# Routed experts of a decoder block: VectorE's split of the next gate weights moves behind the low part of the inner activations

## The reference, cut to what matters

```
router_logits = x_flat @ gate_w.T
top_w, sel = jax.lax.top_k(router_logits, TOPK)          # TOPK = 2, E = 8
top_w = jax.nn.softmax(top_w, axis=-1)
g = jnp.einsum('nd,efd->enf', x_flat, gate_proj)         # D = 512, F_DIM = 352
u = jnp.einsum('nd,efd->enf', x_flat, up_proj)
h = jax.nn.silu(g) * u
eo = jnp.einsum('enf,edf->end', h, down_proj)
out = jnp.einsum('end,ne->nd', eo, tw)
```

## Time and profile before

| | value |
|---|---|
| profiled execution | 3482.6 us, of which the span of the core 3480.8 us |
| median of three timed runs | 3479.44 us (3477.32 to 3481.93) |
| TensorE matmul busy over the span | 3159.6 us (91%) |
| VectorE, ScalarE, GpSimd busy | 2094.4 (60%), 1278.2 (37%), 1450.4 us (42%) |
| mean granted TensorE clock | 0.955 of full speed |
| stretch of the routed experts of layer 1 | about 3075 to 3412 us from the span's start |

### The profile page before, as it was taken

One profiled execution on the slowest core, in us unless ns is written; L12 is line 12 of the kernel. 1 busy time (PEld: TensorE's weight loads), 2 busy tenths in 40 slices (PEclk: granted clock), 3 DMA queues, 4 the chain that ended last, 5 costly groups with the idle time before them and its releaser, 6 DMA issues. The chain is left out here.

```text
span 3480.8 us, 58860 instructions
## 1 busy us (share of the span) xinstructions
PE 3159.6 (91%) x21152; PEld 2638.6 (76%) x21152; DVE 2094.4 (60%) x3767; ACT 1278.2 (37%) x3276; POOL 1450.4 (42%) x1470
## 2 busy tenths in 40 slices
PE   7999999999969999799896999699999999869991
PEld 6887878878847777678685777488888888758881
DVE  5666566576645776421064777556667678645656
ACT  3333333333346666201102333244444444324430
POOL 4454343344422434300153222355555556544445
PEclk9999999999989999789998999799999999979996
DMA  4001016022310111339563112211101001156665
GB/s 172 18 16 51 0 35 232 0 95 102 141 33 24 53 32 57 144 100 340 171 143 115 37 42 63 99 56 34 36 12 47 12 24 43 39 199 223 225 221 157
DMA packets 137872, 317.18 MB, mean 91 GB/s; under 512 B 18425, under 2 KB 30457, under 8 KB 135538
## 3 DMA queue, kind: packets, MB, share of 16 engines
q1 hardware_dynamic: 120194, 274.61, 23.4%
q0 software_dynamic: 15360, 36.25, 3.9%
q10 hardware_dynamic: 2160, 4.21, 0.4%
HBM read 231.07 MB, written 98.04 MB: 95 GB/s over the span
## 5 line engine op out<-in xcount | busy, mean ns | idle before, releaser
L398 POOL TENSOR_TENSOR a_sq<-a_tq,a_sinq 128x256 f32<-128x256 f32 x128 | 150.3, 1194 | 358.4 <-DVE a_tq L474 358.4
L398 POOL TENSOR_TENSOR a_sk<-a_tk,a_sink 128x256 f32<-128x256 f32 x128 | 123.8, 986 | 90.0 <-DVE a_tk L474 90.0
L364 ACT COPY a_probT<-bank 128x512 f32<-128x512 f32 x64 | 37.6, 587 | 328.3 <-PE bank L713 328.3
L411 POOL TENSOR_TENSOR e_sk<-e_tk 128x512 f32<-128x512 f32 x64 | 66.6, 1040 | 204.6 <-DVE e_tk L501 204.6
L353 ACT ACTIVATE e_prob<-bank,e_nb,e_rq 128x128 f32<-128x128 f32 x256 | 113.9, 455 | 86.7 <-DVE e_nb L575 86.7
L348 ACT ACTIVATE a_sm<-a_sm,a_nmax 128x128 f32<-128x128 f32 x256 | 99.8, 391 | 121.7 <-DVE a_nmax L570 121.7
L952 ACT ACTIVATE b_prob<-bank,b_nb 128x128 f32<-128x128 f32 x512 | 139.4, 387 | 11.6 <-DVE b_nb L1148 11.3
L1046 POOL TENSOR_TENSOR d_prob<-d_prob,d_nmax 128x1024 f32<-128x1024 f32 x32 | 64.0, 1999 | 183.3 <-DVE d_nmax L1143 183.3
L2340 POOL TENSOR_TENSOR n_wu_lo<-nw_wu,n_wu_hi 128x1408 fp32r<-128x1408 f32 x23 | 74.0, 3218 | 135.4 <-DVE n_wu_hi L2384 135.4
L496 DVE TENSOR_TENSOR a_kr<-a_kr,a_sk 128x512 f32<-128x512 f32 x64 | 66.4, 1037 | 89.0 <-POOL a_sk L398 89.0
L1145 DVE TENSOR_REDUCE b_nmax<-bank 128x8 f32<-128x1024 f32 x64 | 77.9, 1217 | 68.6 <-PE bank L1289 67.9
(11 more groups left out here) (512 smaller groups left out, 10718.8 us busy)
## 6 DMA issues: line engine op xcount, KB each, us to landing
packed<-all_zero SPq DMA_DIRECT2D x32, 1024.0 KB, 8.3
cw_wg<-in_c_wg SPq DMA_DIRECT2D x32, 512.0 KB
cw_wu<-in_c_wu SPq DMA_DIRECT2D x32, 512.0 KB
cw_wd<-in_c_wd SPq DMA_DIRECT2D x32, 512.0 KB
nw_wg<-in_f_wg SPq DMA_DIRECT2D x23, 704.0 KB
nw_wu<-in_f_wu SPq DMA_DIRECT2D x23, 704.0 KB
nw_wd<-in_f_wd SPq DMA_DIRECT2D x23, 512.0 KB
nw_xe<-packed SPq DMA_DIRECT2D x46, 256.0 KB, 2.7
```

The costliest lines, as they stand in the source:

```text
L364: nc.scalar.copy(probT[:], pP[:, :]).then_inc(act_pt, 1)
L398: step = nc.gpsimd.tensor_tensor(o, i, s, ALU.mult)
```

## The change

VectorE's list for an odd slot is put in another order. Before: `take_x`, `split_gate`, `take_h`, h. After: `take_x`, `take_h`, `split_gate`, h. Even slots have no `split_gate` and stay as they are, as do all other engines, all buffers and all semaphores. In slot 0, which has no `take_h`, and in the last odd slot, which has no `split_gate`, nothing moves.

```diff
@@ -2387,10 +2387,10 @@
                 t = R * i + n
                 if ahead:
                     take_x(*following(i, n, R))
+                if back:
+                    take_h(*preceding(i, n, R))
                 if n % 2 and not (isinstance(i, int) and later(i, n) > LAST):
                     split_gate(*((i, 1) if n == 1 else (i + 1, 0)))
-                if back:
-                    take_h(*preceding(i, n, R))
                 dve.wait_ge(act_g, done(t))
                 dve.wait_ge(pe_u, done(t))
                 nc.vector.tensor_tensor(h[:, n % 2], gate[:, n % 2], pU[n % 2][:, 0:F], ALU.mult).then_inc(v_h, 1)
```

## The result

The changed kernel takes 3463.66 us (median of 6 runs, 3454.95 to 3465.68) where the kernel before, timed beside it, takes 3483.06 us (6 runs, 3477.32 to 3485.33). The ratio is 0.9943, with an interval of 0.993 to 0.9957: **faster by 0.57%, about 20 us**. The forecast was 3460 us; 3459.7 over 3479.44 is the same ratio, 0.9943. In microseconds the forecast lies 3.7 us under the median, since the kernel before came out 3.6 us slower in six runs than in the three of the forecast.

The account below looks back on a forecast made before the run. TensorE was taken to bound the routed experts, held in odd slots by the low part of h; 16.4 + 4.7 - 1.4 = 19.7 us off 3479.44 gave 3460 us, with 3455 to 3469 for 8 in 10.

Parts of the forecast that it names:

- The bound and the term of 16.4 us: Routed experts: TensorE sets the pace; odd slots from slot 3 on shrink to 6.685 us like even ones, gaining 16.4 us.
- Slots 1 and 2, 4.7 us: Start of the routed stage: a 2.8 us wait and the low clock behind it vanish, gaining 4.7 us, at least 2.8.
- The split costs nothing behind GpSimd's order: Odd slots: the gate-weight split at T+4.1 starts 0.96 us ahead of GpSimd's down-weight instruction, keeps the port, costs nothing.
- an L2379 of 1.6 to 1.9 us: Sign on VectorE in odd slots: the gate-weight split starts at T+4.1 and takes 1.6 to 1.9 us.
- the slack of 1.2 us: Margin between the split's end at T+5.7 to 5.8 and TensorE's need of it at T+7.0, next even slot.
- Rival B: Split falls behind GpSimd's down weights at the port and the gate product waits: 3500 us, or 3528; chance 0.07.
- the first case of B: Split stands still for GpSimd's first instruction only; gate product waits 1.9 us in 22 even slots: 42 us lost, 3500 us.
- The loss of 1.4 us to the loads: Loop of up-weight load, high part, y copy, store, next load: late landings give back 1.4 us.
- the ends of 0 and 4.8: Bounds of the loss to late loads: 0 at best, 4.8 us if all eleven unseen landings came at their bound.
- its cases, which were 4.8 and 1.5: Loss to loads if eleven landings came at their bound (4.8 us) or 0.3 us earlier (1.5 us).
- Rival A: Loads set the pace: each landing takes 8.3 us, 20 pairs lose 0.55 us each after 2 us: 3467 us; chance 0.14.
- Rival C: No difference: odd slots are long for another reason; gain under 5 us, 3475 to 3479 us; chance 0.07.

Follow-up runs that it names:

- a1: The changed kernel run again with nothing else altered; ratio to the kernel before 0.9939, slots 3 to 43 in 273.88 us.
- e2: The changed kernel with SyncE issuing the loads for the pair after next ahead of a store; ratio to the kernel before 0.9934.
- e9: The changed kernel with the earlier loads of e2, run a second time; ratio to the kernel before 0.9935.
- e4: The kernel before with the new order in the odd slots n = 1 alone; ratio to the kernel before 0.9985.
- e5: The kernel before with the new order in the odd slots n = 3 alone; ratio to the kernel before 0.9983.
- a2: The kernel before run again with nothing altered; ratio 1.000, slots 1 and 2 in 19.49 us.
- e1: The changed kernel with the split of the gate weights moved one place further back, behind the product h; ratio to the kernel before 1.0065.
- a3: The changed kernel run a third time with nothing else altered; ratio to the kernel before 0.9946, slots 3 to 43 in 277.27 us.
- e3: The kernel before, VectorE's order as it was, with only the earlier loads of e2; ratio to the kernel before 0.9977.
- e8: The kernel of e4 with the earlier loads of e2; ratio to the kernel before 0.9953.
- e7: The changed kernel with SyncE loading 48 KB into a spare tensor and awaiting it before each pair's weights; ratio to the kernel before 0.9958.

## Why the prediction was right, point by point

**The bound and the term of 16.4 us.** Right. TensorE's odd slots went to 6.68 us in the first profile, all but two, and the gross term (41 slots at the floor) is met to 0.2 us in a1, e2 and e9: 273.88 for 274.1.

**Slots 1 and 2, 4.7 us.** Right: 18.03 became 13.36. That the whole 4.7 us hang on the order in slot 1 is shown by e4 and e5. The clock part is seen in the profile after. The first stretch lies where the old hole was (T+4.8 to T+7.6), the second where the stretch of the earlier trace rows with a clock of 0.61 was (T+7.6 to T+11.6); both have 1.00 (columns as there):

```profile
3081.00:3085.00 4.00, 4.00 (x25) 3.56 (x24) 3.96 (x5) 1.47 (x3) 4.00 (x2) 1.00 1.00 409
3084.50:3088.50 4.00, 4.00 (x28) 3.94 (x27) 1.67 (x5) 2.47 (x5) 2.79 (x2) 1.00 0.43 164
```

These 4.7 us are a quarter of the whole gain, and the list of waits has only 2.8 of them. That it was 4.7 and no more is in part luck: the text had nothing above 4.7, and a2 has 6.1 over the floor.

**The split costs nothing behind GpSimd's order.** Right for a load in time: it started at T+4.0 to 4.1, took 1.61 us and held L2345 up by 0.5 us. But the sign that the text named, an L2379 of 1.6 to 1.9 us, came in seven of 21 slots only; in the other 14 the split was 2.1 to 3.2 us long behind a late L2340, and the slack of 1.2 us paid for most of it. Slot 19 above has the 1.49 us behind L2340 that slot 17 and slot 39 had shown before. The rule of the Trainium skill on the lock ("SBUF — State Buffer", section "SBUF: two separate sides"), by which the one that starts first keeps the pair of ports for its whole instruction, is borne out by e1, with L2345 first: the split ends 1.47 us behind L2345's first instruction, and its second 1.15 us behind the split, which is about what each needs alone (1.61 and 1.25 us). Rival B, which lived on that order, is e1: 0.3 us after GpSimd costs 47 us over the floor, 0.96 us before it nothing. The forecast for the first case of B was right in the hole, 1.97 for 1.9 us, and had left out the clock behind it.

**The loss of 1.4 us to the loads.** The mechanism was right and the size was off by a factor of two: 2.9 us in the profile (3.4 in a3, 0 in a1). It was within the ends of 0 and 4.8. VectorE waited for 18 of 20 loads, and the stall began where the text had it, when L2340 ends after about T+5.5: at T+5.39 (a3) nothing is lost, at T+5.94 (slot 19) 0.52 us. The text puts 1.4 "between the last two" of its cases, which were 4.8 and 1.5; it lies under both. What was mis-sized is less the mean landing than the count made with it. The mean from issue to use is 7.89 us, between two cases of the text, 7.82 without a loss and 7.93 with 1.5. But the landings are not spread evenly. The nine loads used from slot 7 to slot 23 took 8.24 us on average, and all of the loss lies in slots 11 to 24; the other eleven took 7.60, and a load that comes early gives nothing back. A second, small path was not in the text: in slot 11 L2384 is so late (T+2.23) that the low part of h, behind it on VectorE, is late too, and with slot 15 that makes 0.5 of the 2.9 us.

**The total.** The parts in the profile are 16.61 + 4.67 - 2.94 = 18.3 us for the stage, where the text had 19.7; the timed runs give 19.4. That the ratio agrees to four digits is luck, as its interval, 0.993 to 0.9957, is 9 us wide.

**Rival A** (the loads set the pace) is half true: the period is 13.50 us in the profile after, 0.14 over the floor, and the sign that the text named for it, TensorE held by `n_wg_lo` behind a late L2340, is there in five even slots. But its landing of 8.3 us for every load did not come: six of the last 20 took so long, the mean is 7.89. **Rival C** is ruled out by the odd slots.

**What the prediction did not see** is why the odd slots of before were 0.37 to 1.67 us too long, and not 0.37 each. It had no reserve against a late load: with the split waiting for L2340 and the low part of h behind both, each late load went straight to TensorE (e3), and a slot made shorter made the next load late (e4, e5, e8). The new order puts some 2.6 us of reserve there (L2340 ends at T+2.8 with a load in time, and may end at T+5.4). The sum came out since it took all odd slots down at once; for half of the slots the same way of adding predicted 8.4 us in slots 3 to 43 for e4, and 0.3 were measured.

## What to carry to other kernels

Where two engines keep a port from each other, look at who asks first, and put the instruction for which another engine waits soonest ahead of the one that may be stopped; a start 1.2 us later, from 0.97 us ahead of the other engine to 0.24 us behind it, was worth 1.2% here (e1 against the changed kernel). Gains of single stretches add up only if no loop goes through them: ask, for each stretch that is made shorter, which load was issued in the one before and when it is wanted. Issuing loads as soon as their buffer is free, and not behind a store that waits for the slowest engine, took away what was left and made the stage the same in both traces.

## What the runs showed of the hardware that was not expected

- The same hole of TensorE is not always the same price: in e1 TensorE is idle for 1.7 us in each even slot from 4 on, and this is followed by a granted clock of 0.57 to 0.61 over the next 4 us in five slots (10.2 us) and by 1.00 in fifteen (8.65 us). The hole of 2.8 to 3.0 us in slot 1 lowered the clock in both traces of the kernel before, but cost 4.7 us in one and 6.1 in the other. What decides stays open.
- GpSimd's two instructions of L2345, back to back on its queue, let a waiting VectorE instruction in between: 5.0 us in place of 3.65.
- How long a load takes from issue to landing is not a matter of its size alone: 704 KB of up weights took 7.6 to 8.0 us on average when issued right behind the x loads (after, a1, a3), and 5.75 us in e7, where SyncE waited for a small load in between.
